# Attention over 32 heads: weighing the values in two halves of 256 columns, and the maxima seven steps ahead

## The chip, the core and the metric

The kernel is one program on one core of a Trainium2 chip. The metric is the device time of that program in microseconds (us). The core has five engines that run side by side and meet only at semaphores: TensorE (matmuls; PE in the rows, and PEld for its weight loads), VectorE (DVE), ScalarE (ACT), GpSimd (POOL) and SyncE (SP), which here issues the transfers. Matmuls write into PSUM, whose eight banks hold 512 float32 columns each.

## What is computed

Three layers follow each other on x of shape 2 x 2048 x 128: half a mixture-of-experts layer, attention with 16 heads of 8 dimensions in each of the 2 batches, and the mixture again. The change is in the attention:

```python
q = _rms_norm(q, q_norm_w); k = _rms_norm(k, k_norm_w)
q = _apply_rope(q, rope_cos, rope_sin); k = _apply_rope(k, rope_cos, rope_sin)
q = q / math.sqrt(HEAD_DIM)
scores = jnp.einsum('bqhd,bkhd->bhqk', q, k)
attn = jax.nn.softmax(scores.astype(jnp.float32), axis=-1)
out = jnp.einsum('bhqk,bkhd->bqhd', attn, v).reshape(b, s, HIDDEN)
return out @ wo.T
```

There are 32 heads (16 in each batch), each with 2048 queries and 2048 keys.

## The kernel before

`attention_phase` goes through the heads one after the other. A head is cut into 16 tiles of 128 keys (`KT`) and 4 chunks of 512 queries (`CHUNKS`, `BLK`). The softmax needs the maximum of each query's scores before it can take exponentials, so every score is computed twice. For the maxima the scores lie with queries on the partitions; for the weighing they lie with keys on the partitions.

A *step* g of a head is the inner loop of `turn` on TensorE. It issues, in this order, four pairs made of one scores matmul (`scores`, L1205; `pe_next`, L1250, for the first tile of the next head) and one maxima matmul (`maxima`, L1187), and then the weighing (`weigh`, L1215) of the key tile of the step before. The names used below are S0 to S3 for the scores of the four chunks, M0 to M3 for the maxima matmuls, and W for the weighing.

- S writes into a ring of three PSUM banks (`SRING`). ScalarE takes exponentials from there (`exps`, L1144) into `at_prob`, four a step. Sc may start once the exponential three entries earlier is done (`free`). So S3 waits for the exponential of S0 of its own step.
- M writes pairs of banks (`MRING` = 2 pairs). VectorE takes the maximum over each pair, 1024 columns at a time (`reduce`, L1275), two a step, 32 a head. M0 waits for the reduction of the pair two pairs earlier; so does M2.
- W multiplies the values of one key tile (`vals`, 128 x 32 float32, of which 8 columns are values and one gives the sum) by `at_prob`. Chunk c goes to the partitions 32c to 32c+31 of one bank, so that four matmuls of 512 columns work in four column groups of the array side by side. The bank O gathers all 16 tiles of a head. Each float32 matmul of the program is two matmul records in the trace, with a weight load each.

The maxima run ahead of the weighing. `LAG` = 11: in the steps 1 to 11 of head h TensorE issues the maxima of the tiles 5 to 15 of head h+1, and from step 12 on those of the tiles 0 to 4 of head h+2. When the last maxima of head h+1 are reduced, VectorE takes the maximum over the pairs and negates it (L1289), GpSimd splits it in three bfloat16 parts (`split`, L1071 to L1077), TensorE turns these (`turn_maxima`, L1200) at the end of step `TURN_MAXIMA` = 13, ScalarE copies them to `at_mrows` (L1155) and SP moves them into the rows of `q_head` that S reads with the others (`place_maxima`, L1104). The first S of the next head, in step 16, waits for that transfer.

At the end of a head ScalarE copies the bank O to `at_sums` (`keep_sums`, L1149) as soon as the last weighing is done. The first weighing of the next head waits for this copy. SP loads head h+3 and stores the sums of head h after the last weighing of head h. Before step 1 of head 0 there is a prologue with all 64 maxima matmuls of head 0 and the first 20 of head 1. In head 30 no maxima are left after step 11, and head 31 has none; in its steps 8 to 15 it also holds the output projection of the first batch.

Of the kernel before, what the change touches and what calls it, by code (L numbers as in the profile page):

```python
# [24 lines left out]
BLK = 512  # L25
# [11 lines left out]
HD1 = HD + 1  # L37
BH = BATCH * HEADS
PATCH = 508
KT = SEQ // P  # L40
LN_EPS, RMS_EPS = 1e-5, 1e-6
BUFS = 3
PROBS = 4
# [949 lines left out]
def attention_phase(nc, sem, kept, ps, v, identb, q, k, vals, q_rows, k_rows, qk_loaded, qk_stored,  # L993
# [9 lines left out]
    CHUNKS = SEQ // BLK  # L1003
    STEPS = KT * CHUNKS
    PAIRS_OF_HEAD = STEPS // 2
    ENTRIES = STEPS + 1
    AHEAD, LAG = 2, 11
    TURNS = BH - AHEAD
    SRING = 3
    MRING = 2  # L1010
    VSTEPS = 4
    TURN_MAXIMA = LAG + 2
    OUT_FROM = KT - 2 * BPS
    assert TURNS % BUFS == 0 and BUFS * ENTRIES % SRING == 0 and PAIRS_OF_HEAD % MRING == 0
    max_scored = sem("at_max_scored")
# [27 lines left out]
    with ExitStack() as tmp:  # L1043
# [56 lines left out]
        @block.sync  # L1100
        def _(sp):
            def place_maxima(h, i):
                sp.wait_ge(exped, turned_at(h) + 1)
                sp.dma_start(q[i][MROW:MROW + MR, :], mrows[:]).then_inc(max_placed, 16)  # L1104

            def store_sums(h):
                sp.wait_ge(sums_kept, h + 1 + PRIME)
                for c in range(CHUNKS):
                    cols = slice(c * BLK, (c + 1) * BLK)
                    sp.dma_start(sum_rows[h][:, cols], sums[32 * c:32 * c + HD1, :]).then_inc(sums_stored, 16)  # L1110

            def turn(h, i):
                place_maxima(h + 1, (i + 1) % BUFS)
                sp.wait_ge(weighed, (h + 1) * KT + PRIME)
                load_head(sp, q[i], k[i], q_rows[h + BUFS], k_rows[h + BUFS], qk_loaded[i])
                store_sums(h)

            prime(sp, sums_stored)
            for h in range(1, BUFS):
                load_head(sp, q[h], k[h], q_rows[h], k_rows[h], qk_loaded[h])  # L1120
            for i in range(2):
                sp.wait_ge(qk_stored[i], 16 * NB)
            place_maxima(0, 0)
            for it in range(0, BH // BUFS - 1):
                for i in range(BUFS):
                    turn(it * BUFS + i, i)
            for h in range((BH // BUFS - 1) * BUFS, BH):
                if h < BH - BUFS:
                    turn(h, h % BUFS)
                else:  # L1130
                    if h < BH - 1:
                        place_maxima(h + 1, (h + 1) % BUFS)
                    store_sums(h)
                if h == BH - 2:


                    load_sums(sp, 0, sum_rows, o, den, o_loaded[0])
# [42 lines left out]
        def _(pe):  # L1180
# [24 lines left out]
                pe.matmul(ps[:, S + bank(i, g, c, last), :], k[i][0:KS, g * P:(g + 1) * P],  # L1205
                          q[i][0:KS, c * BLK:(c + 1) * BLK], start=True, stop=True).then_inc(scored, 1)

            def weigh(h, i, g, last=False):

                pe.wait_ge(exped, entry(h, g, CHUNKS - 1, last) + 1)  # L1210
                if g == 0:
                    pe.wait_ge(values_placed, h + 1)
                    pe.wait_ge(sums_kept, h + PRIME)
                for c in range(CHUNKS):
                    last = pe.matmul(ps[32 * c:32 * c + 32, O, :], vals[i][:, g, :], prob[:, g % PROBS, c, :],  # L1215
                                     start=(g == 0), stop=(g == KT - 1), skip_group_check=True)
                last.then_inc(weighed, 1)

            def turn(h, i, loads=None, last=False):

# [2 lines left out]
                for g in range(1, KT + 1):  # L1223
# [4 lines left out]
                    for c in range(CHUNKS):  # L1228
# [4 lines left out]
                        if g <= LAG and not last:  # L1233
                            maxima(h + 1, nxt, (KT - LAG + g - 1) * CHUNKS + c)
                        elif g > LAG and loads is not None:
                            maxima(h + AHEAD, far, (g - LAG - 1) * CHUNKS + c)
                    if g == TURN_MAXIMA and not last:
                        turn_maxima(h + 1, nxt, turned_bank(i + 1))
                    weigh(h, i, g - 1, last)
                    if last and OUT_FROM <= g < KT:  # L1240
                        blk, part = divmod(g - OUT_FROM, 2)
                        if part == 0:
# [198 lines left out]
```

## Time and profile before

| | |
|---|---|
| median of 3 runs | 2074.75 us (2071.16 to 2346.2) |
| the profiled execution, its own time | 2068.4 us |
| its span | 2066.6 us |
| busy share of the span: PE, DVE, ACT, POOL | 89%, 74%, 63%, 16% |
| granted TensorE clock in the heads 1 to 30 | 1.00 of 2.4 GHz |
| maxima reductions (L1275) | 1024 of 1220 ns mean, 1206.5 us busy |
| exponentials (L1144) | 2048 of 604 ns mean, 1057.0 us busy |
| weighing matmuls (L1215) | 4096 records of 606 ns mean, 546.5 us busy |

A busy share is an average over the whole span. The attention heads take about 1,290 of the 2,066 us, and they are one pattern that repeats every step and every head, so it is read from a single step and a single head. Records of TensorE overlap: a matmul's duration includes its way through the array, and the distance from start to start says how long it holds the array.

### The profile page before, as it was taken

The page shows a single profiled execution, that of the slowest core. Times are in us where ns is not written, and L with a number is a line of the kernel's source. Part 1 is how long each engine was busy: PE and PEld are TensorE (multiplying, and loading weights), DVE is VectorE, ACT ScalarE, POOL GpSimd, SP SyncE. Part 2 cuts the span into 40 slices and gives each one's busy share as a digit, 9 for nine tenths or more (in the row PEclk, how much of TensorE's full clock was granted, in tenths as well). Part 3 has the DMA queues.
Part 4 walks back from the last instruction along what each step waited for, and adds up shares of the span by engine and source line. Part 5 has one row for each costly group of instructions (what it writes and reads, how often), then busy time and mean ns, then how long its engine had stood idle before and what let it go on. Part 6 is the DMA issues. An engine that isn't in the chain of part 4 may idle for free. (4 is left out here: it accounts for less than half of the span.)

```text
span 2066.6 us, 28460 instructions
## 1 busy us (share of the span) xinstructions
PE 1849.4 (89%) x10619; PEld 702.0 (34%) x10619; DVE 1520.4 (74%) x1691; ACT 1297.2 (63%) x2497; POOL 335.9 (16%) x408
## 2 busy tenths in 40 slices
PE   4799997689999999999999999999999997679998
PEld 2466655512222222222222222222222222456665
DVE  6333335599999999999999999999999972533333
ACT  3222223518888888888888888888888886222222
POOL 2355550300000000000000000000000000035554
PEclk9899996759999999999999999999999999689999
DMA  4543310300000000000000000000000001068462
GB/s 107 117 127 111 111 43 16 126 28 18 18 18 30 22 18 21 32 18 18 31 22 18 22 31 18 18 31 21 18 23 30 18 3 30 20 122 131 118 116 61
DMA packets 65155, 98.23 MB, mean 48 GB/s; under 512 B 12013, under 2 KB 31026, under 8 KB 65018
## 3 DMA queue, kind: packets, MB, share of 16 engines
q1 hardware_dynamic: 60858, 94.32, 18.0%
q10 hardware_dynamic: 4160, 2.10, 0.4%
q8 instruction: 84, 1.38, 0.3%
q14 instruction: 53, 0.43, 0.1%
HBM read 84.94 MB, written 11.04 MB: 46 GB/s over the span
## 5 line engine op out<-in xcount | busy, mean ns | idle before, releaser
L1275 DVE TENSOR_REDUCE at_mx<-ps 128x1 f32<-128x1024 f32 x1024 | 1206.5, 1220 | 78.1 <-PE ps L1187 39.8
L1144 ACT ACTIVATE at_prob<-ps 128x512 f32<-128x512 f32 x2048 | 1057.0, 604 | 215.4 <-PE ps L1205 203.1
L1187 PE MATMUL ps<-k_head,q_head 48*128 48x512 bf16 x2048 | 711.0, 395 | 20.4 <-PEq L779 14.1
L1205 PE MATMUL ps<-q_head,k_head 51*128 51x512 bf16 x1924 | 581.9, 383 | 75.0 <-ACT at_prob L1144 33.2
L1215 PE MATMUL ps<-at_prob,vals 128*32 128x512 f32 x4096 | 546.5, 606 | 0.0
L688 DVE TENSOR_TENSOR e_hidden<-e_part,ps 128x512 f32<-128x512 f32 (+1 forms) x208 | 143.2, 688 | 323.0 <-POOL e_part L665 318.2
L1205 PEld LDWEIGHTS ps<-q_head,k_head 51*128 51x128 bf16 x1924 | 143.4, 94 | 684.9 <-ACT at_prob L1144 574.1
L639 ACT ACTIVATE e_silu<-ps 128x512 f32<-128x512 f32 (+1 forms) x208 | 124.2, 597 | 323.1 <-PE ps L597 323.1
L665 POOL TENSOR_TENSOR e_part<-e_silu,e_cw 128x512 f32<-128x512 f32 (+1 forms) x208 | 264.5, 1272 | 366.1 <-ACT e_silu L639 200.7
L1187 PEld LDWEIGHTS ps<-k_head,q_head 48*128 48x128 bf16 x2048 | 151.2, 94 | 193.0 <-DVE at_mx L1275 176.3
L605 PE MATMUL ps<-e_hidden,wdown 128*128 128x512 f32 (+1 forms) x416 | 214.5, 598 | 2.0 <-DVE e_hidden L688 2.0
L1071 POOL TENSOR_TENSOR at_mparts<-at_neg,at_zero 128x16 bf16<-128x16 f32 x32 | 7.0, 220 | 984.8 <-DVE at_neg L1289 984.8
L597 PE MATMUL ps<-xnT_hi,wgate_hi 128*128 128x512 f32 x208 | 148.6, 714 | 10.7 <-DVE e_hidden L688 7.6
L1215 PEld LDWEIGHTS ps<-at_prob,vals 128*32 128x32 f32 x4096 | 80.9, 108 | 111.5 <-issue 108.1
L605 PEld LDWEIGHTS ps<-e_hidden,wdown 128*128 128x128 f32 (+1 forms) x416 | 77.5, 189 | 25.4 <-DVE e_hidden L688 9.8
L597 PE MATMUL ps<-xnT_hi,wgate_lo 128*128 128x512 f32 x208 | 82.9, 399 | 0.0
L597 PE MATMUL ps<-xnT_lo,wgate_hi 128*128 128x512 f32 x208 | 81.9, 394 | 0.0
L597 PE MATMUL ps<-xnT_hi,wup_hi 128*128 128x512 f32 x192 | 76.3, 397 | 0.0
L597 PE MATMUL ps<-xnT_hi,wup_lo 128*128 128x512 f32 x192 | 76.0, 396 | 0.0
L597 PE MATMUL ps<-xnT_lo,wup_hi 128*128 128x512 f32 x192 | 75.1, 391 | 0.0
L597 PEld LDWEIGHTS ps<-xnT_hi,wgate_hi 128*128 128x128 f32 x208 | 39.5, 190 | 71.8 <-issue 49.6
L597 PEld LDWEIGHTS ps<-xnT_lo,wgate_hi 128*128 128x128 f32 x208 | 39.7, 191 | 35.2 <-issue 35.1
(171 smaller groups left out, 896.9 us busy)
## 6 DMA issues: line engine op xcount, KB each, us to landing
e_cw<-comb_rows SPq DMA_DIRECT2D x80, 256.0 KB, 4.2
e_cw<-comb_rows SPq DMA_DIRECT2D x32, 224.0 KB, 5.9
e_cw<-comb_rows SPq DMA_DIRECT2D x32, 192.0 KB, 5.0
q_head<-q_rows SPq DMA_DIRECT2D x64, 96.0 KB
k_head<-k_rows SPq DMA_DIRECT2D x64, 96.0 KB
e_cw<-comb_rows SPq DMA_DIRECT2D x32, 160.0 KB, 4.5
e_cw<-comb_rows SPq DMA_DIRECT2D x48, 96.0 KB, 3.5
e_cw<-comb_rows SPq DMA_DIRECT2D x32, 128.0 KB, 6.1
```

The source lines that it names most:

```text
L597: last = pe.matmul(ps[:, bank + i, :], w[wp][:, cols], xnT[xp][:, tokens], start=(m == 0), stop=(m == len(PASSES) - 1))
L605: pe.matmul(ps[:, Y, :], wdown[0:rows[c], c, :], hidden[0:rows[c], (par + c) % 2, :], start=(c == 0), stop=(c == CH - 1)).then_inc(downed, 1)
L639: act.activation(silu[0:rows[c], i, :], ps[0:rows[c], GATE + i, :], ACT.Silu).then_inc(silued, 1)
L665: pool.tensor_tensor(part[0:rows[c], i, :], silu[0:rows[c], i, :], cw[0:rows[c], c, :], ALU.mult).then_inc(weighted, 1)
L688: dve.tensor_tensor(hidden[0:rows[c], i, :], part[0:rows[c], i, :], up, ALU.mult).then_inc(hidden_ready, 1)
L1071: pool.tensor_tensor(mparts[i][:, 0, :], neg[i][:], zero[:], ALU.add).then_inc(max_split, 1)
L1144: act.activation(prob[:, g % PROBS, c, :], ps[:, S + bank(i, g, c, last), :], ACT.Exp).then_inc(exped, 1)
L1187: one = pe.matmul(ps[:, at, :], q[i][HALF:HALF + KR, (j // CHUNKS) * P:(j // CHUNKS + 1) * P], k[i][HALF:HALF + KR, c * BLK:(c + 1) * BLK] ...
L1205: pe.matmul(ps[:, S + bank(i, g, c, last), :], k[i][0:KS, g * P:(g + 1) * P], q[i][0:KS, c * BLK:(c + 1) * BLK], start=True, stop=True).th ...
L1215: last = pe.matmul(ps[32 * c:32 * c + 32, O, :], vals[i][:, g, :], prob[:, g % PROBS, c, :], start=(g == 0), stop=(g == KT - 1), skip_grou ...
L1275: dve.tensor_reduce(mx[i][:, j // 2, j % 2:j % 2 + 1], ps[:, at:at + 2, :].rearrange("p a t -> p (a t)"), AX.X, ALU.max).then_inc(max_redu ...
```

## The change

Each weighing becomes two halves. Half 0 is issued after the second pair of the step and half 1 at its end, where the whole weighing stood. Half 0 takes the chunks 0 and 1, half 1 the chunks 2 and 3. A chunk is cut in two pieces of 256 columns, and the four pieces of a half go to the four column groups, so a half is again four matmuls side by side, each of 256 columns instead of 512. In the bank O half 0 has the columns 0 to 255 of the four groups and half 1 the columns 256 to 511. Half 0 waits for the exponential of chunk 1 of the tile before, half 1 for that of chunk 3; only half 1 tells the others that the tile is weighed. The first half 0 of a head carries the wait for `at_sums`.

`store_sums` still issues four transfers, now of 256-column pieces, to put the columns back in order. `LAG` goes from 11 to 9, so that seven tiles (0 to 6) of the maxima run two heads ahead instead of five, and the prologue has 28 maxima matmuls of head 1 instead of 20. `TURN_MAXIMA` is `LAG` + 3 = 12, one step earlier than before and three steps behind the last maxima of the next head instead of two.

```diff
-    AHEAD, LAG = 2, 11
+    AHEAD, LAG = 2, 9
-    TURN_MAXIMA = LAG + 2
+    HALF_BLK = BLK // 2
+    TURN_MAXIMA = LAG + 3
@@
-                for c in range(CHUNKS):
-                    cols = slice(c * BLK, (c + 1) * BLK)
-                    sp.dma_start(sum_rows[h][:, cols], sums[32 * c:32 * c + HD1, :]).then_inc(sums_stored, 16)
+                halves = sum_rows[h].rearrange("d (a j t) -> j d a t", a=2, j=4)
+                for j in range(4):
+                    sp.dma_start(halves[j], sums[32 * j:32 * j + HD1, :].rearrange("d (a t) -> d a t", a=2)).then_inc(sums_stored, 16)
@@
-            def weigh(h, i, g, last=False):
-                pe.wait_ge(exped, entry(h, g, CHUNKS - 1, last) + 1)
-                if g == 0:
+            def weigh(h, i, g, half, last=False):
+                pe.wait_ge(exped, entry(h, g, 2 * half + 1, last) + 1)
+                if g == 0 and half == 0:
                     pe.wait_ge(values_placed, h + 1)
                     pe.wait_ge(sums_kept, h + PRIME)
-                for c in range(CHUNKS):
-                    last = pe.matmul(ps[32 * c:32 * c + 32, O, :], vals[i][:, g, :], prob[:, g % PROBS, c, :],
-                                     start=(g == 0), stop=(g == KT - 1), skip_group_check=True)
-                last.then_inc(weighed, 1)
+                for j in range(4):
+                    done_one = pe.matmul(ps[32 * j:32 * j + 32, O, half * HALF_BLK:(half + 1) * HALF_BLK], vals[i][:, g, :],
+                                         prob[:, g % PROBS, 2 * half + j // 2, j % 2 * HALF_BLK:(j % 2 + 1) * HALF_BLK],
+                                         start=(g == 0 and half == 0), stop=(g == KT - 1), skip_group_check=True)
+                if half == 1:
+                    done_one.then_inc(weighed, 1)
@@
+                        if c == 1:
+                            weigh(h, i, g - 1, 0, last)
                     if g == TURN_MAXIMA and not last:
                         turn_maxima(h + 1, nxt, turned_bank(i + 1))
-                    weigh(h, i, g - 1, last)
+                    weigh(h, i, g - 1, 1, last)
```

TensorE's order in a step of head 0, before. L1205 rows are S, L1187 rows M, and L1215 rows W:

```order
L1205 MATMUL ps<-q_head0,k_head0 128x512 [waits at_exped]
L1187 MATMUL ps<-k_head1,q_head1 128x512
L1205 MATMUL ps<-q_head0,k_head0 128x512 [waits at_exped]
L1187 MATMUL ps<-k_head1,q_head1 128x512 [waits at_max_reduced]
L1205 MATMUL ps<-q_head0,k_head0 128x512 [waits at_exped]
L1187 MATMUL ps<-k_head1,q_head1 128x512
L1215 MATMUL ps<-at_prob,vals0 32x512 [waits at_sums_kept,at_values_placed,at_exped]
L1215 MATMUL ps<-at_prob,vals0 32x512 x3
```

The same place in the changed kernel (its lines stand one further on), from S1 and M1 to the end of the step:

```order
L1206 MATMUL ps<-q_head0,k_head0 128x512 [waits at_exped]
L1188 MATMUL ps<-k_head1,q_head1 128x512
L1216 MATMUL ps<-at_prob,vals0 32x256 [waits at_sums_kept,at_values_placed,at_exped]
L1216 MATMUL ps<-at_prob,vals0 32x256 x3
L1206 MATMUL ps<-q_head0,k_head0 128x512 [waits at_exped]
L1188 MATMUL ps<-k_head1,q_head1 128x512 [waits at_max_reduced]
L1206 MATMUL ps<-q_head0,k_head0 128x512 [waits at_exped]
L1188 MATMUL ps<-k_head1,q_head1 128x512
L1216 MATMUL ps<-at_prob,vals0 32x256 [waits at_exped]
L1216 MATMUL ps<-at_prob,vals0 32x256 x3
```

Four matmuls of 256 columns now stand between the second and the third pair, with the wait for `at_sums` on the first of them, and four more where the four of 512 columns stood. The second place is the end of the step that turns the maxima, on TensorE, before:

```order
L1205 MATMUL ps<-q_head0,k_head0 128x512 [waits at_exped]
L1187 MATMUL ps<-k_head2,q_head2 128x512
L1200 MATMUL ps<-identb,at_mparts1 48x128 [waits at_max_split,at_exped]
L1215 MATMUL ps<-at_prob,vals0 32x512 [waits at_exped]
L1215 MATMUL ps<-at_prob,vals0 32x512 x3
```

And in the changed kernel:

```order
L1206 MATMUL ps<-q_head0,k_head0 128x512 [waits at_exped]
L1188 MATMUL ps<-k_head2,q_head2 128x512
L1201 MATMUL ps<-identb,at_mparts1 48x128 [waits at_max_split,at_exped]
L1216 MATMUL ps<-at_prob,vals0 32x256 [waits at_exped]
L1216 MATMUL ps<-at_prob,vals0 32x256 x3
```

Here only the distance from the last maxima of head 1 has changed, from two steps to three, and what follows the turned matmul is half a weighing. The order of the work on ScalarE and GpSimd is as before but for that one step; VectorE's order is the same.

## Rows read from the trace of the kernel before

**Rows 1.** Windows view, heads 1 to 30: stretch, us, busy by engine, clock, DMA.
```profile
500.00:1660.00 1160.00, 1077.24 (x7433) 256.55 (x7431) 1092.80 (x955) 973.16 (x1910) 33.77 (x145) 1.00 0.07 23
```

**Rows 2.** Timeline of one step: start, duration, engine, line, operation, count, idle before.
```profile
1000.29 0.39 PE L1205 MATMUL ps<-q_head,k_head 51*128 51x512 bf16 x1
...
1000.51 0.38 PE L1205 MATMUL ps<-q_head,k_head 51*128 51x512 bf16 x1
1000.52 0.38 PE L1187 MATMUL ps<-k_head,q_head 48*128 48x512 bf16 x1
...
1000.77 2.06 ACT L1144 ACTIVATE at_prob<-ps 128x512 f32<-128x512 f32 x4 [0.39 <-PE ps L1205]
...
1001.42 0.39 PE L1205 MATMUL ps<-q_head,k_head 51*128 51x512 bf16 x1
...
1001.74 1.06 PE L1215 MATMUL ps<-at_prob,vals 128*32 128x512 f32 x8
...
1002.74 0.39 PE L1205 MATMUL ps<-q_head,k_head 51*128 51x512 bf16 x1
```

**Rows 3.** Timeline of VectorE in two short stretches around the same step.
```profile
1000.96 1.22 DVE L1275 TENSOR_REDUCE at_mx<-ps 128x1 f32<-128x1024 f32 x1
```
```profile
1000.96 2.36 DVE L1275 TENSOR_REDUCE at_mx<-ps 128x1 f32<-128x1024 f32 x2
```

**Rows 4.** Timeline of VectorE over one head.
```profile
972.96 0.18 DVE L1289 TENSOR_REDUCE at_neg<-at_mx 128x16 f32<-128x32 f32 x1
973.14 2.35 DVE L1275 TENSOR_REDUCE at_mx<-ps 128x1 f32<-128x1024 f32 x2
976.29 9.71 DVE L1275 TENSOR_REDUCE at_mx<-ps 128x1 f32<-128x1024 f32 x8 [0.80 <-PE ps L1187]
986.24 26.89 DVE L1275 TENSOR_REDUCE at_mx<-ps 128x1 f32<-128x1024 f32 x22 [0.24 <-PE ps L1187]
```

**Rows 5.** Timeline of PE, head 31: a weighing's two sets, in two short stretches.
```profile
1734.01 0.64 PE L1215 MATMUL ps<-at_prob,vals 128*32 128x512 f32 x4
```
```profile
1734.46 0.61 PE L1215 MATMUL ps<-at_prob,vals 128*32 128x512 f32 x4
1735.00 0.38 PE L1332 MATMUL ps<-woT,at_oT 128*128 128x128 f32 x1
```

**Rows 6.** Windows view of two dense stretches of TensorE; columns as in the first group.
```profile
361.40:364.80 3.40, 3.35 (x30) 3.25 (x30) 2.56 (x5) 2.82 (x7) 2.40 (x2) 1.00 0.01 2
1001.42:1001.80 0.38, 0.38 (x6) 0.15 (x10) 0.38 (x1) 0.38 (x2) 0.00 (x0) 1.00 0.00 0
```

**Rows 7.** Timeline, late in one head: turned maxima, copy of the sums, last load.
```profile
974.47 0.22 PE L1200 MATMUL ps<-identb,at_mparts 128*48 128x128 bf16 x1 [0.48 <-POOL at_mparts L1077]
...
982.98 0.39 PE L1205 MATMUL ps<-q_head,k_head 51*128 51x512 bf16 x1
...
983.11 0.60 ACT L1149 ACTIVATE at_sums<-ps 128x512 f32<-128x512 f32 x1
```
```profile
990.04 0.28 SPq L977 DMA_DIRECT2D k_head<-k_rows  x1
```

**Rows 8.** Timeline of VectorE in the prologue.
```profile
424.24 25.94 DVE L1275 TENSOR_REDUCE at_mx<-ps 128x1 f32<-128x1024 f32 x22
450.10 0.17 DVE L1289 TENSOR_REDUCE at_neg<-at_mx 128x16 f32<-128x32 f32 x1
450.19 4.70 DVE L1275 TENSOR_REDUCE at_mx<-ps 128x1 f32<-128x1024 f32 x4
```

**Rows 9.** Timeline of ScalarE: first exponentials of step 1, heads 0, 1, 30, 31.
```profile
464.39 2.06 ACT L1144 ACTIVATE at_prob<-ps 128x512 f32<-128x512 f32 x4 [1.63 <-PE ps L1205]
```
```profile
502.32 2.06 ACT L1144 ACTIVATE at_prob<-ps 128x512 f32<-128x512 f32 x4
```
```profile
1665.85 2.06 ACT L1144 ACTIVATE at_prob<-ps 128x512 f32<-128x512 f32 x4
...
1705.56 2.06 ACT L1144 ACTIVATE at_prob<-ps 128x512 f32<-128x512 f32 x4
```

## The prediction, made before the changed kernel ran

> **What bounds the kernel now.** I read the windows view first, to see whether the heads are one pattern and at which clock. From 500 to 1660 us VectorE is busy for 94%, TensorE for 93% and ScalarE for 84% of the time, at the full granted clock of 1.00 [rows 1]. Three engines are nearly full, so no busy share names the bound. The reader has to go to one step and ask of each engine what ended its last wait.
>
> The timeline of one step shows a closed loop through TensorE and ScalarE. S0 starts at 1000.29 and its exponential at 1000.77, 0.48 us later, after 0.39 us in which ScalarE had nothing to do. S3 starts at 1001.42, 0.65 us after that exponential began, because it needs the bank that the exponential frees. W starts at 1001.74, 0.32 us after S3, and the next S0 at 1002.74, 1.00 us after W [rows 2]. The sum is 0.48 + 0.65 + 0.32 + 1.00 = 2.45 us, which is exactly the distance from S0 to S0. So the step is bound by this loop. ScalarE's own work is less: four exponentials take 2.06 us and follow each other at (2.06 - 0.60)/3 = 0.49 us, so 1.95 us a step. The duration of one, 0.60, is read from the copy of the same shape [rows 7].
>
> VectorE is close behind. One reduction takes 1.22 us and two take 2.36 us from the first start to the last end [rows 3], so the second starts 1.14 us after the first when nothing holds it up. Two of them are 2.28 us a step, against the loop's 2.45. The rest is short waits for M. Over a head the timeline shows two bigger ones, 0.80 us and 0.24 us [rows 4], and a head takes (1665.85 - 502.32)/29 = 40.12 us [rows 9]. If VectorE never waited, a head would take 32 x 1.14 + 0.09 for the final maximum (450.10 to 450.19 [rows 8]) = 36.6 us.
>
> **What the split costs TensorE.** The array's time goes by distances from start to start. A pair (S and M side by side, 1000.51 and 1000.52) holds it for 0.22 us (1000.29 to 1000.51 [rows 2]). A weighing has two sets of four records. The second set starts 0.45 us after the first (1734.01, 1734.46) and what comes behind it 0.54 us later (1735.00) [rows 5]. At 2.4 GHz, the clock of these rows, 512 columns twice over are 0.43 us. So the first set costs 0.43 + 0.02, the second 0.43 + 0.11, and going from M3 to W costs 0.32 where a pair costs 0.22, another 0.10.
>
> With 256 columns the streaming part of each set halves to 0.21 us and the rest stays. A half is then 0.24 + 0.33 = 0.57 us, with 0.10 ahead of it. The step is pair 0.22, pair with the way into a weighing 0.32, half 0.57, and the same again: 2 x (0.22 + 0.32 + 0.57) = 2.22 us. As it stands, without waits, it would be 3 x 0.22 + 0.32 + 1.00 = 1.98 us. The split therefore adds 0.24 us of array time to each step. It is hidden as long as 2.22 is less than what VectorE needs, 2.28.
>
> The Trainium skill (TensorEngine Tiling (Array Packing), section Key Properties) says that a change of the tiling mode drains the engine, which speaks against this change, since S and M use half the rows each and W four column groups: two changes a step become four. The trace agrees that a change costs something, 0.10 us each way here. If each of the two added changes cost a matmul's whole way through the array, 0.18 us (the 0.39 us of a record of 512 columns less 0.21 of streaming [rows 2]), the step would be 2.22 + 2 x 0.08 = 2.38 us and TensorE the bound, about 2022 us in all by the reckoning of the first rival below; by the rows it is 2.22.
>
> **What the split removes.** W was one piece of 1.00 us between S3 and the next S0, inside the loop. Now S3 comes 0.22 + 0.32 + 0.57 + 0.22 = 1.33 us after S0, and needs its exponential, done 0.48 + 0.65 = 1.13 us after S0. The wait is gone, and it stays gone by 0.20 us. What is left of the loop on TensorE is its own order, 2.22 us. Then VectorE is late next: M0 starts about 0.05 us after the reduction that frees its banks ends, M1 0.22 later, it takes 0.39, and after 0.05 more its own reduction can start, 0.71 in all. (0.05 is taken from M1, which ends at 1000.52 + 0.38 = 1000.90, and its reduction, which starts at 1000.96 [rows 2, 3].) Counted from the start of the first reduction that is 1.22 + 0.71 = 1.93 us, and VectorE is free for it after 2 x 1.14 = 2.28. So 0.35 us of lateness on TensorE cost VectorE nothing. TensorE makes up 1.14 - 1.11 = 0.03 us in every half step, which is 1 us in a head.
>
> **What comes once a head.** The turned maxima waited 0.48 us for GpSimd and cost VectorE most of its 0.80 [rows 4, 7]; with three steps instead of two they are ready before TensorE asks, and 0.2 to 0.3 us of array time remain. That is within the 0.35. The first half weighing of a head now stands 0.54 us behind S0, while the copy of the sums starts 0.13 us behind that S0 (983.11 against 982.98) and takes 0.60 [rows 7]; with 0.05 for the signal it lets TensorE go at 0.78. So a new wait of 0.24 us appears on TensorE; behind it queue S2, M2, S3, M3, and VectorE waits for these. It too is within the 0.35. If that cover were gone, the two would cost 0.5 us a head, 15 us in all. Loads: SP's last one of a head is issued at 990.04 [rows 7], 7 us into the head; it is wanted in step 10, more than 20 us in, where it was step 12. The four stores of the sums are four still. Nothing for either.
>
> **The ends.** Head 0 runs from 464.39 to 502.32, heads 1 to 29 from there to 1665.85, head 30 to 1705.56 [rows 9]. The prologue gets four more reductions, at (25.94 - 1.22)/21 = 1.18 us each [rows 8]: +4.7 us. Head 0: 37.9 to 36.6, -1.3. Heads 1 to 29: 1163.5 to 29 x 36.6 = 1061.4, -102.1. Head 30: 39.7 to 9 x 2.28 + 7 x 2.22 = 36.1, -3.6. Head 31 has no M, so only TensorE's 2.22 against 2.45 in 16 steps: -3.7. What LAG itself brings is the 4.7 us in front and the 0.48 us of waiting; it moves reductions and saves none.
>
> **The sum**: 4.7 - 1.3 - 102.1 - 3.6 - 3.7 = -106 us. From the profiled execution's own 2068.4 us that gives 1962; that execution lay 0.3% under the median of 2074.75, the lowest run at 2071. I add 4 us for small hold-ups that I have no row for, and say 1966.
>
> **The rivals.** *The halves cost more than the rows say.* No row shows four column groups with 256 columns, whose weights (four loads a set) have 0.21 us instead of 0.43 to get in. The margin is only 0.03 us per half. Beyond it TensorE is the bound, and each 0.01 us more per half is 0.32 us a head, 10 us in all. With 0.05 more a head is 16 x 2.32 = 37.1 plus about 0.5 for the two waits above, now uncovered: 37.6, and the time 1995. At 0.12 more the gain is nothing. For it speaks that the margin is thin; against it that the same array takes single records of 128 columns every 0.11 us with full weights, 30 matmuls and 30 loads in 3.4 us [rows 6]. The Trainium skill (TensorE: Matmul & The Clock Gate, section Back-to-back issue gap) has matmuls bound by an issue of about 62 ns each in one decode setting. Eight of them would be 0.50 us a half against 0.45 of sets, which is this rival at +0.05, about 1995; no row decides it, since the records wait in a queue.
>
> *TensorE's issue becomes the bound, and the kernel is slower.* A step has 32 records (16 matmuls, 16 loads) now and will have 48. At more than 2.45/48 = 0.051 us for each, sustained, the step is longer than today. The densest long stretch has 60 in 3.4 us, 0.057 each [rows 6]: 48 would be 2.72 us, a head 43.5 and the time 2068 + 31 x 3.4 = 2174. Against it: 16 records are noted in the 0.38 us behind S3's wait, 0.024 each [rows 6], though these may have been queued before; and the 3.4 us hold 30 matmuls of 128 columns twice over, which at 2.4 GHz are 0.107 us each and account for the stretch by streaming.
>
> *The wait moves and the step stays.* If VectorE could not take a reduction every 1.14 us in a row (the rows show two, or four in 4.70 us with one longer distance [rows 8]), but only at the 1.22 of its duration, a head would be 32 x 1.22 + 0.1 = 39.1 and the time about 2068 - 31 = 2037. Against it: 22 in 25.94 us in the prologue, 1.18 each.
>
> **How the numbers follow.** As forecast, bound by VectorE, 1950 to 1980: 0.62. Halves dearer by 0.01 to 0.1, 1980 to 2045: 0.20. Reductions not at 1.14, 2000 to 2040: 0.07. Issue-bound and slower, 2070 to 2180: 0.07. Something unseen that keeps the time as it is: 0.04. The likeliest case alone is 1950 to 1980. The range goes to 2035, which leaves out the slower rival, no change and the worst of the dearer halves, about 0.15. Its low end is VectorE at 1.13 us a reduction, 10 us less, and no hold-ups. 2%, 41 us, is about what can be told from no change, so faster means under about 2033: 0.62 + 0.16 + 0.04 = 0.82; same 0.10; slower 0.08.
>
> **What would show it.** In the profile after: S0 to S0 is 2.28 to 2.30 us; VectorE over 98% busy in the heads, its reductions 1.14 us apart in long rows; S3 no longer waits for the exponential, M does wait for the reductions, which is where its idle time goes; half weighings 0.24 + 0.33 us. I am wrong if the sets of a half lie further apart, if VectorE still has a gap in each step, or if the wait for `at_sums` reaches VectorE.

## The result, and the profile after

The changed kernel takes 1964.13 us (median of 4 runs, 1960.59 to 1968.55), the kernel before 2072.95 us in the same series. The ratio is 0.9486 with a 95% interval of 0.9452 to 0.952; it leaves out one slow execution of the kernel before, 2346.2 us. The forecast was 1966 us with a range of 1950 to 2035. The profiled execution took 1963.15 us with a span of 1961.4, against 2066.6 before.

From the head of the page of the changed kernel: busy time, share and instructions of each engine, then VectorE's busy share and TensorE's granted clock in tenths over 40 slices:

```profile
span 1961.4 us, 36652 instructions
PE 1818.1 (93%) x14715; PEld 716.9 (37%) x14715; DVE 1477.8 (75%) x1691; ACT 1335.2 (68%) x2497; POOL 336.1 (17%) x408
...
DVE  6333335679999999999999999999999933623333
...
PEclk9899997856999999999999999999999997699999
```

The windows view over its heads (stretch, us, busy us and count of PE, PEld, DVE, ACT, POOL, then clock, DMA share and GB/s), the counterpart of [rows 1]:

```profile
500.00:1560.00 1060.00, 1047.49 (x11199) 269.78 (x11197) 1057.77 (x960) 1012.54 (x1920) 33.95 (x145) 1.00 0.08 25
```

VectorE is busy for 99.8% of this stretch where it was busy for 94%. TensorE went from 93 to 99% and ScalarE from 84 to 96%. All three are nearly full, so again the busy shares do not say which one decides. The timeline of VectorE does:

```profile
966.29 0.17 DVE L1294 TENSOR_REDUCE at_neg<-at_mx 128x16 f32<-128x32 f32 x1
966.39 36.44 DVE L1280 TENSOR_REDUCE at_mx<-ps 128x1 f32<-128x1024 f32 x32
1002.75 0.17 DVE L1294 TENSOR_REDUCE at_neg<-at_mx 128x16 f32<-128x32 f32 x1
1002.84 36.44 DVE L1280 TENSOR_REDUCE at_mx<-ps 128x1 f32<-128x1024 f32 x32
1039.20 0.17 DVE L1294 TENSOR_REDUCE at_neg<-at_mx 128x16 f32<-128x32 f32 x1
```

All 32 reductions of a head stand in one row without a gap. Over the whole stretch from 500 to 1560 us the view of L1280 has VectorE waiting for TensorE once, for 0.28 us (ahead of the row at 1054.35). One takes (36.44 - 1.21)/31 = 1.136 us from start to start, and a head takes 1039.20 - 1002.75 = 36.45 us. Before, the same row was broken by waits of 0.80 and 0.24 us and by short ones in each step [rows 4].

TensorE's timeline shows the half step that replaces the long piece of [rows 2]:

```profile
1009.88 0.39 PE L1206 MATMUL ps<-q_head,k_head 51*128 51x512 bf16 x1
1009.88 0.39 PE L1188 MATMUL ps<-k_head,q_head 48*128 48x512 bf16 x1
1010.11 0.38 PE L1206 MATMUL ps<-q_head,k_head 51*128 51x512 bf16 x1
1010.11 0.38 PE L1188 MATMUL ps<-k_head,q_head 48*128 48x512 bf16 x1
1010.42 0.64 PE L1216 MATMUL ps<-at_prob,vals 128*32 128x256 f32 x8
1010.99 0.39 PE L1206 MATMUL ps<-q_head,k_head 51*128 51x512 bf16 x1
```

The distances are 0.23, 0.31 and 0.57 us, together 1.11. In this half step TensorE catches up behind the turned maxima's matmul (1005.77) and waits for nothing. Where it has caught up, the distance grows to 1.13 or 1.14, because M then waits for a reduction. S0 to S0 is thus 2.21 to 2.27 us, a little under the 2.28 to 2.30 that I had named. S3 no longer waits: the list of TensorE's waits from 500 to 1560 us has no exponential left, where it had 24.0 us in 85 waits of S before.

The time went as follows, by stretches of the two profiled executions. The bounds of the heads are the ScalarE rows that answer to [rows 9].

| stretch | before | after | difference | forecast |
|---|---|---|---|---|
| start to the first final maximum (450.10, 452.68) | 450.1 | 452.7 | +2.6 | 0 |
| from there to 464.39 and 471.81 | 14.3 | 19.1 | +4.8 | +4.7 |
| rest of head 0 | 37.9 | 34.1 | -3.9 | -1.3 |
| heads 1 to 29 | 1163.5 | 1057.4 | -106.2 | -102.1 |
| head 30 | 39.7 | 36.2 | -3.5 | -3.6 |
| head 31, to the copy of its sums | 45.5 | 42.1 | -3.4 | -3.7 |
| from there to the end | 315.5 | 319.9 | +4.4 | 0 |
| span | 2066.6 | 1961.4 | -105.2 | -106 |

The rows of ScalarE for the changed kernel from which the table is made:

```profile
471.81 24.60 ACT L1145 ACTIVATE at_prob<-ps 128x512 f32<-128x512 f32 x44 [0.88 <-PE ps L1206]
...
505.86 1.10 ACT L1145 ACTIVATE at_prob<-ps 128x512 f32<-128x512 f32 x2
```
```profile
1563.21 1.10 ACT L1145 ACTIVATE at_prob<-ps 128x512 f32<-128x512 f32 x2
...
1599.40 1.10 ACT L1145 ACTIVATE at_prob<-ps 128x512 f32<-128x512 f32 x2
...
1641.54 0.60 ACT L1150 ACTIVATE at_sums<-ps 128x512 f32<-128x512 f32 x1 [1.82 <-PE ps L1216]
```

### The profile page after: what moved, and what is told of

It is laid out like the page before. It is cut to its first block and busy times, and to the rows that moved or that the text cites. A ratio compares the mean times of both kernels' runs of the same rounds, so it can differ in the third digit from the quotient of the medians.

```text
span 1961.4 us, 36652 instructions
## 1 busy us (share of the span) xinstructions
PE 1818.1 (93%) x14715; PEld 716.9 (37%) x14715; DVE 1477.8 (75%) x1691; ACT 1335.2 (68%) x2497; POOL 336.1 (17%) x408
## 5 line engine op out<-in xcount | busy, mean ns | idle before, releaser
L1280 DVE TENSOR_REDUCE at_mx<-ps 128x1 f32<-128x1024 f32 x1024 | 1165.9, 1214 | 9.6 <-PE ps L1188 7.6
L1145 ACT ACTIVATE at_prob<-ps 128x512 f32<-128x512 f32 x2048 | 1097.7, 595 | 67.3 <-PE ps L1206 22.5
L1216 PE MATMUL ps<-at_prob,vals 128*32 128x256 f32 x8192 | 655.0, 391 | 13.4 <-ACT at_sums L1150 13.4
L1188 PE MATMUL ps<-k_head,q_head 48*128 48x512 bf16 x2048 | 638.9, 392 | 21.6 <-PEq L779 14.7
L1216 PEld LDWEIGHTS ps<-at_prob,vals 128*32 128x32 f32 x8192 | 162.2, 108 | 427.4 <-ACT at_prob L1145 412.7
L1206 PEld LDWEIGHTS ps<-q_head,k_head 51*128 51x128 bf16 x1924 | 117.6, 93 | 403.7 <-ACT at_prob L1145 388.1
L1188 PEld LDWEIGHTS ps<-k_head,q_head 48*128 48x128 bf16 x2048 | 120.0, 94 | 62.5 <-DVE at_mx L1280 44.8
L1064 POOL COPY vals<-v 128x128 f32<-128x128 f32 x32 | 9.2, 292 | 332.5 <-PE ps L1216 332.5
```

The lines of the kernel that those rows point to most:

```text
L1064: pool.tensor_copy(vals[i][:, :, 0:HD], head).then_inc(values_placed, 1)
L1145: act.activation(prob[:, g % PROBS, c, :], ps[:, S + bank(i, g, c, last), :], ACT.Exp).then_inc(exped, 1)
L1188: one = pe.matmul(ps[:, at, :], q[i][HALF:HALF + KR, (j // CHUNKS) * P:(j // CHUNKS + 1) * P], k[i][HALF:HALF + KR, c * BLK:(c + 1) * BLK] ...
L1216: done_one = pe.matmul(ps[32 * j:32 * j + 32, O, half * HALF_BLK:(half + 1) * HALF_BLK], vals[i][:, g, :], prob[:, g % PROBS, 2 * half + j ...
L1280: dve.tensor_reduce(mx[i][:, j // 2, j % 2:j % 2 + 1], ps[:, at:at + 2, :].rearrange("p a t -> p (a t)"), AX.X, ALU.max).then_inc(max_redu ...
```

## The experiments

The theory under test has three parts. The step before was a loop through TensorE and ScalarE with the weighing in it. Halving the weighing and moving one half forward opens that loop. What is left is VectorE's pace, with TensorE close behind it because each piece of weighing has a fixed cost. The rivals are that VectorE was the bound already and the gain came from maxima that run further ahead, that short pieces help in themselves, and that moving the weighing would have done without cutting it.

### The halves without the rest, and the rest without the halves

```diff
 split_only, against the changed kernel
-    AHEAD, LAG = 2, 9
+    AHEAD, LAG = 2, 11
...
-    TURN_MAXIMA = LAG + 3
+    TURN_MAXIMA = LAG + 2
 ahead_only, against the kernel before
-    AHEAD, LAG = 2, 11
+    AHEAD, LAG = 2, 9
...
-    TURN_MAXIMA = LAG + 2
+    TURN_MAXIMA = LAG + 3
```

> The changed kernel with LAG and TURN_MAXIMA set back to 11 and 13; only the weighing stays in halves. Theory (the halves take the weighing out of the loop between TensorE and ScalarE, and VectorE's reductions become the bound): nearly the whole gain stays, a head of 36.5 to 36.9 us, in all 1965 to 1972 us: 5 us less in the prologue, but the turned maxima are now wanted about 2.3 us earlier (they were ready 1.7 us before TensorE asked), so TensorE waits some 0.6 us a head, of which VectorE feels 0.2 to 0.4. Rival (the gain is from running the maxima further ahead, so that VectorE is never short): back to 2050 to 2075 us, 40 us a head.

> The kernel before with LAG 9 and TURN_MAXIMA 12 and the weighing in one piece. Theory: the step stays 2.45 us, a head loses at most the 0.48 us for which TensorE waited for the split maxima and the prologue gets 5 us longer: 2060 to 2078 us. Rival (running ahead is the gain): 1965 to 2000 us.

The halves alone took 1981.93 us, ratio 0.9553 (0.953 to 0.9577). The maxima alone took 2063.98 us, 0.9957 (0.9942 to 0.9972), inside the 2060 to 2078 expected. So the halves alone bring 91 us of 109, and the rest brings 9 us by itself (0.4%, small but outside the interval) and 18 us on top of the halves. The 18 are more than I had expected: 1981.93 lies above my 1965 to 1972. The timeline of VectorE with the halves alone:

```profile
942.50 0.17 DVE L1294 TENSOR_REDUCE at_neg<-at_mx 128x16 f32<-128x32 f32 x1
942.59 2.35 DVE L1280 TENSOR_REDUCE at_mx<-ps 128x1 f32<-128x1024 f32 x2
945.40 8.01 DVE L1280 TENSOR_REDUCE at_mx<-ps 128x1 f32<-128x1024 f32 x7 [0.47 <-PE ps L1188]
953.65 26.11 DVE L1280 TENSOR_REDUCE at_mx<-ps 128x1 f32<-128x1024 f32 x23 [0.24 <-PE ps L1188]
979.68 0.17 DVE L1294 TENSOR_REDUCE at_neg<-at_mx 128x16 f32<-128x32 f32 x1
```

and, of the same kernel, a TensorE row from the head before:

```profile
906.83 0.22 PE L1201 MATMUL ps<-identb,at_mparts 128*48 128x128 bf16 x1 [0.77 <-POOL at_mparts L1078]
```

TensorE waits 0.77 us for the split maxima, and VectorE has nothing to do for 0.47 + 0.24 = 0.71 us of the head, which is 37.18 us long. That is 0.73 more than 36.45. Over 30 heads it is 22 us, less 5 us for the shorter prologue 17, against 18 measured. I had expected VectorE to feel only 0.2 to 0.4 us of it.

### Which of the two numbers counts

```diff
 lag11_turn14, against the changed kernel (TURN_MAXIMA stays LAG + 3)
-    AHEAD, LAG = 2, 9
+    AHEAD, LAG = 2, 11
 lag10_turn13, against the changed kernel
-    AHEAD, LAG = 2, 9
+    AHEAD, LAG = 2, 10
```

> The changed kernel with LAG 11 as before the change, and the turned maxima still three steps behind the last maxima, so in step 14. Theory (what mattered of the second part of the change is only the distance of three steps; LAG itself just makes the prologue longer): no wait for the split maxima, 36.45 us a head, and four reductions less ahead of head 0: 1956 to 1962 us, if the transfer of the turned maxima lands before step 16, where it is wanted two steps after it is made instead of four. Rival (that transfer is then late): 0.3 us or more a head lost, 1970 us and up. Rival (maxima seven steps ahead are needed in themselves): as with the halves alone, 1982 us.

> The same between the two: LAG 10, turned maxima in step 13. Theory: 36.45 us a head and two reductions less in the prologue, 1959 to 1964 us. Rival (maxima seven steps ahead are needed in themselves): 1970 us or more.

LAG 11 with the turn in step 14 took 1973.56 us, 0.9521 (0.9505 to 0.9538). LAG 10 with the turn in step 13 took 1963.42 us, 0.9468 (0.9449 to 0.9487), the same as LAG 9. The list of TensorE's waits for LAG 11 (engine, line, waited for: us in all, times, longest) names the reason:

```profile
PE ps L1255 <- DMA q_head<-at_mrows: 10.4, 28, 0.5
```

The wait for the split maxima is gone, but the transfer of the turned maxima now lands late: step 16 waits 10.4/28 = 0.37 us for it. A head takes 37.09 us (final maxima at 932.33 and 969.42). This was the first rival of that run. So LAG is bound from two sides: the turn has to stand three steps behind the last maxima and three ahead of the next head. With 16 steps that makes LAG 10 the largest that fits. LAG 10 gives the same time with six steps ahead, so "seven steps ahead" is not needed in itself.

### Was VectorE the bound before, and is it now?

```diff
 before_short_reduce and after_short_reduce
-                dve.tensor_reduce(mx[i][:, j // 2, j % 2:j % 2 + 1], ps[:, at:at + 2, :].rearrange("p a t -> p (a t)"),
+                dve.tensor_reduce(mx[i][:, j // 2, j % 2:j % 2 + 1], ps[:, at:at + 2, :].rearrange("p a t -> p (a t)")[:, 0:768],
```

> The kernel before with reductions over 768 instead of 1024 columns; the maxima over the left-out 256 columns are not taken. Theory (the step of 2.45 us is the loop of TensorE and ScalarE, and VectorE only stands close behind it): the step stays at 2.45 us, though VectorE has a fifth less to do; at most 0.4 us a head goes from the waits at the turned maxima, and some 5 us in the prologue: 2050 to 2068 us. Rival (VectorE's pace was the bound before as well): 2.0 us a step or a little more, below 1900 us.

> The changed kernel with reductions over 768 instead of 1024 columns; the maxima over the left-out 256 columns are not taken. Theory (VectorE is the bound at 1.14 us per reduction and TensorE stands just behind it at 2.2 us a step): the step falls only to TensorE's own 2.20 to 2.26 us, plus about 0.5 us a head of waits, a head of 35.7 to 36.4 us, in all 1940 to 1960 us. Rival (TensorE has room and VectorE alone is the bound): the step follows the reductions, about 1.75 us or ScalarE's 1.95, a head of 31 to 32 us, 1810 to 1830 us.

The kernel before took 2054.91 us with short reductions, the changed one 1946.39 us (one run each, 2073 in the same series for the kernel as it was). ScalarE's timeline of the kernel before with short reductions shows that the step has not moved at all:

```profile
1001.54 2.07 ACT L1144 ACTIVATE at_prob<-ps 128x512 f32<-128x512 f32 x4 [0.39 <-PE ps L1205]
1003.99 1.58 ACT L1144 ACTIVATE at_prob<-ps 128x512 f32<-128x512 f32 x3 [0.39 <-PE ps L1205]
```

It is 2.45 us as before, with the same 0.39 us of waiting for S0, although VectorE now waits 0.57 us in each step. A head is 39.73 us. VectorE was not the bound. In the changed kernel the head goes from 36.45 to 36.16 us only:

```profile
918.41 0.18 DVE L1294 TENSOR_REDUCE at_neg<-at_mx 128x16 f32<-128x32 f32 x1
...
954.57 0.17 DVE L1294 TENSOR_REDUCE at_neg<-at_mx 128x16 f32<-128x32 f32 x1
```

With VectorE out of the way TensorE's rows stand 2.21 us a step apart, 16 x 2.21 = 35.4 us; the other 0.8 us come once a head, from the wait for `at_sums` and the turned maxima's matmul. So VectorE is the bound now by 0.3 us in 36, and a faster VectorE would bring no more than that in a head.

### The place and the size of the pieces

```diff
 whole_middle, against the kernel before
+                        if c == 1:
+                            weigh(h, i, g - 1, last)
...
-                    weigh(h, i, g - 1, last)
 halves_end, against the changed kernel
-                        if c == 1:
-                            weigh(h, i, g - 1, 0, last)
...
+                    weigh(h, i, g - 1, 0, last)
                     weigh(h, i, g - 1, 1, last)
```

> The kernel before with the weighing in one piece, but issued after the second pair instead of at the end of the step. Theory (what counts is that the weighing no longer stands between S3 and the next S0; the halves cost 0.24 us of array time on top): the old loop is gone, another opens, S3 to its exponential 0.49, the exponential 0.60, 0.05 to the weighing of the next step, 1.00 for it and 0.22 for S2, 2.36 us a step, so a head of about 38 us and 2000 to 2015 us in all. Rival (two short pieces are what helps, since one long piece keeps VectorE short wherever it stands): 2.45 us a step or more, 2060 us and up.

> The changed kernel with both halves at the end of the step, one behind the other: the pieces stay, their place is undone. Theory (the gain is that the time between S3 and the next S0 is shorter by the first half): the old loop is back and its weighing a little longer, 0.48 + 0.65 + 0.32 + 3 x 0.24 + 0.33 = 2.50 us a step, about 0.8 us a head more than with the maxima ahead alone: 2080 to 2105 us. Rival (shorter pieces help in themselves): below 2000 us.

Both halves at the end took 2071.16 us (one run, the kernel before 2069.98 beside it). The gain is gone, so shorter pieces do nothing by themselves. But the time lies below my 2080 to 2105: I had the halves in a row too dear. TensorE's rows put sixteen records where eight were:

```profile
1003.01 1.07 PE L1216 MATMUL ps<-at_prob,vals 128*32 128x256 f32 x16
1004.02 0.39 PE L1206 MATMUL ps<-q_head,k_head 51*128 51x512 bf16 x1
```

From the start of the weighing to the next S0 it is 1.01 us, against 1.00 for one piece [rows 2]; I had expected 1.05. The four sets of the sixteen records start at 1003.01, 1003.25, 1003.47 and 1003.68, so from the second on a set costs 0.22 and 0.21 us, its streaming alone. Twice as many matmuls and weight loads one behind the other cost nearly nothing. The step is 2.46 us and the head 39.80, against 39.72 with the maxima ahead alone, where I had expected 0.8 us more.

The whole weighing in the middle took 2123.36 us, ratio 1.0261 (1.0221 to 1.0301). It is slower than the kernel before, and my 2000 to 2015 was wrong. TensorE and ScalarE over one step:

```profile
1003.21 0.39 PE L1205 MATMUL ps<-q_head,k_head 51*128 51x512 bf16 x1
...
1003.63 2.06 ACT L1144 ACTIVATE at_prob<-ps 128x512 f32<-128x512 f32 x4 [0.66 <-PE ps L1205]
...
1004.77 1.06 PE L1215 MATMUL ps<-at_prob,vals 128*32 128x512 f32 x8
...
1005.77 0.39 PE L1205 MATMUL ps<-q_head,k_head 51*128 51x512 bf16 x1
```

S2 starts at 1003.21 and its exponential 0.42 us later. The exponential of S3 has to queue behind it, 0.49 later, and takes 0.60; 0.05 later the weighing of that tile may start, which takes 1.00 until the next S2. That is 0.42 + 0.49 + 0.60 + 0.05 + 1.00 = 2.56 us, the distance from 1003.21 to 1005.77. I had let the exponential of S3 start 0.49 us after S3 and forgotten that ScalarE was still at the one before. The whole weighing needs the exponential of chunk 3, the last of the step, and in the middle of the next step that is a tight wait. This shows what the cut is for: half 0 needs only the chunks 0 and 1, which are ready long before the middle, so it can stand there. It does not show that cutting is the only way. A whole weighing in the middle, but of the tile before that one, should find all its exponentials done, and `at_prob` has room for four tiles; no run tried it.

### The price of a piece

```diff
 quarters, against the changed kernel (sums stored and copied to match)
-                pe.wait_ge(exped, entry(h, g, 2 * half + 1, last) + 1)
+                pe.wait_ge(exped, entry(h, g, half, last) + 1)
...
-                                         prob[:, g % PROBS, 2 * half + j // 2, j % 2 * HALF_BLK:(j % 2 + 1) * HALF_BLK],
+                                         prob[:, g % PROBS, half, j * QUARTER:(j + 1) * QUARTER],
...
-                        if c == 1:
-                            weigh(h, i, g - 1, 0, last)
+                        if c < 3:
+                            weigh(h, i, g - 1, c, last)
 quarters_from_head_2: the same where this is 4, halves where it is 2
+    def pieces(h):
+        return 4 if h >= 2 else 2
 three_pieces: half 0 as it is, the chunks 2 and 3 as quarters behind the third and the fourth pair
...
-                        if c == 1:
-                            weigh(h, i, g - 1, 0, last)
+                        if c in (1, 2):
+                            weigh(h, i, g - 1, c - 1, last)
```

> The changed kernel with the weighing in four quarters of 128 columns per column group, one behind each pair. Theory (each piece has fixed costs that do not shrink with its columns: 0.10 us into it, 0.02 between its sets, 0.11 out of it): a quarter is 0.32 + 0.13 + 0.22 = 0.67 us from pair to pair, the step 2.68 us and TensorE the bound by far, with the waits once a head 43.5 us a head, 2170 to 2195 us in all. First rival (the costs shrink with the columns): still VectorE's 36.5 us a head, 1965 us. Second rival (four weight loads no longer get in beside 0.11 us of streaming): each quarter longer by 0.1 us or more, 2230 us and up.

> The changed kernel with its second half cut in two quarters of 128 columns, one behind the third pair and one behind the fourth; SP stores the sums in eight transfers instead of four. Theory (each piece has fixed costs, 0.24 us, and the clock stays up): 0.22 + 0.32 + 0.57 + 2 x (0.32 + 0.35) = 2.45 us a step, TensorE the bound, 39.8 us a head, 2055 to 2085 us. Rival (costs shrink with the columns): 1965 us. Rival (with more and shorter pieces the granted clock stays at 0.50 as with the quarters): near 4 us a step, above 2700 us.

> Quarters as in the run before, but only from head 2 on; heads 0 and 1 are weighed in halves, so that the clock has risen to 1.00 before the first quarter. Theory A (the half clock of the quarters' run was only never left): the clock holds, the step is 2.68 us and the head 43.5 us, 2160 to 2185 us. Theory B (the quarters' pattern itself takes the clock down): it falls to 0.50 within head 2, the step goes to 4.5 us, above 2900 us.

The quarters took 3123.83 us. That is in the range of the second rival (2230 us and up), but not for its reason, and none of the three theories foresaw what happened. The windows view tells it; the third number from the end of a row is the granted clock:

```profile
480.00:500.00 20.00, 20.00 (x181) 5.45 (x180) 11.03 (x9) 10.75 (x18) 0.00 (x0) 0.50 0.00 1
...
1000.00:2000.00 1000.00, 996.28 (x8824) 271.80 (x8822) 540.94 (x455) 536.00 (x909) 16.30 (x70) 0.50 0.04 13
```

The clock read 0.50 (1.2 GHz) in the prologue, as in the kernels before and after the change, and it stayed there until late in head 31, with TensorE busy for 99.6% of the long stretch. It rose at last in the steps that also hold the output projection, behind the third group of its matmuls (L1337; the groups at 2766.21 and 2779.07 had not raised it), and the quarters that followed kept it:

```profile
2791.93 2.08 PE L1337 MATMUL ps<-woT,at_oT 128*128 128x128 f32 x8
```
```profile
2790.00:2794.00 4.00, 4.00 (x27) 2.35 (x26) 0.00 (x0) 1.19 (x2) 0.00 (x0) 0.50 0.00 0
...
2795.00:2800.00 5.00, 5.00 (x60) 1.79 (x56) 1.76 (x5) 3.44 (x7) 0.00 (x0) 1.00 0.00 0
```

In the changed kernel the clock rises soon after the first weighing:

```profile
465.00:470.00 5.00, 4.71 (x22) 0.83 (x22) 3.44 (x3) 3.20 (x7) 0.00 (x0) 0.50 0.01 3
```
```profile
470.00:475.00 5.00, 5.00 (x50) 1.15 (x48) 4.17 (x4) 4.08 (x8) 0.00 (x0) 0.84 0.00 0
475.00:480.00 5.00, 5.00 (x60) 1.27 (x56) 5.00 (x6) 4.80 (x10) 0.00 (x0) 1.00 0.00 0
```

With quarters from head 2 on the kernel took 2198.53 us. The clock was 1.00 when they began and held at 1.00:

```profile
600.00:1700.00 1100.00, 1085.38 (x15957) 406.31 (x15955) 977.64 (x823) 963.54 (x1644) 29.12 (x125) 1.00 0.07 22
```

So theory A of that run was right about the clock: the pattern of quarters does not take it down, but started at 0.50 it did not get up from there in 31 heads. The time is 13 us above theory A's 2160 to 2185. Only one run of each stands behind this, on two different chips; that the clock rose within the first of the two runs, with quarters before and behind, speaks against the chip as the cause. What raised it is not shown. Now the price of a piece can be read at the full clock, in TensorE's timeline of the same kernel:

```profile
1000.51 0.43 PE L1223 MATMUL ps<-at_prob,vals 128*32 128x128 f32 x8
1000.87 0.39 PE L1211 MATMUL ps<-q_head,k_head 51*128 51x512 bf16 x1
1000.87 0.39 PE L1193 MATMUL ps<-k_head,q_head 48*128 48x512 bf16 x1
1001.18 0.42 PE L1223 MATMUL ps<-at_prob,vals 128*32 128x128 f32 x8
```

A quarter is 0.36 us to the next pair and 0.31 from there to the next quarter, together 0.67 to 0.68, where 0.67 was expected. The step is 2.71 us and the head 44.20, 0.7 more than expected. Three pieces took 2079.09 us, within the 2055 to 2085 expected; their head is 40.03 us and TensorE's step 2.46.

The fixed cost can be put together from the three sizes. From a piece's start to the next pair it is 1.00 us with 512 columns, 0.57 with 256 and 0.36 with 128. Streaming is 0.85, 0.43 and 0.21 of that, so 0.14 to 0.15 remain each time. With two halves in a row they are paid once. Together with the 0.10 on the way in, a piece that stands apart costs 0.24 us, and it belongs to the change between pairs and weighing, not to the number of matmuls.

### A variant from these

```diff
 lag10_two_queues, against the changed kernel
-    AHEAD, LAG = 2, 9
+    AHEAD, LAG = 2, 10
...
+                store_groups(sp, h, range(2) if h == BH - 1 else range(4))
...
+            act.wait_ge(sums_kept, BH + PRIME)
+            store_groups(act, BH - 1, range(2, 4))
```

> LAG 10 with the turned maxima in step 13, and the last head's sums stored by two engines, two groups each (SP and ScalarE), since the four stores in a row take SP 3.20 us at the end of the attention where they took 1.35. Theory: 36.45 us a head as in the changed kernel, two reductions less ahead of head 0 (2.4 us) and 1 to 1.6 us less between the last copy of the sums and the reciprocal: 1958 to 1962 us. Rival (the transfers' own time and not their issue sets that distance): no gain at the end, 1962 to 1965 us.

It took 1961.55 us, ratio 0.9474 (0.9459 to 0.949). That is 2.6 us below the changed kernel's median, but the two intervals overlap, so it is not shown to be faster. The distance it was made for did shrink. The stores of the last head in the changed kernel, and the two parts in this one:

```profile
1642.17 3.20 SPq L1111 DMA_DIRECT2D sum_rows<-at_sums  x4
...
1653.84 3.35 DVE L1376 RECIPROCAL at_inv<-at_den 64x512 f32<-64x512 f32 x1 [11.73 <-DMA op_o_second<-sum_rows]
```
```profile
1641.93 1.61 SPq L1044 DMA_DIRECT2D sum_rows<-at_sums  x2
1641.93 2.45 ACTq L1044 DMA_DIRECT2D sum_rows<-at_sums  x2
...
1652.54 3.35 DVE L1382 RECIPROCAL at_inv<-at_den 64x512 f32<-64x512 f32 x1 [10.67 <-DMA op_o_second<-sum_rows]
```

From the first store to the reciprocal it is 11.67 us in the changed kernel and 10.61 here, 1.1 us less.

## Why the prediction was right, step by step

**The loop.** Right, and shown: with VectorE relieved of a quarter of its columns the old step stays at 2.45 us, and with both halves back at the end it is 2.46.

**The half weighing.** 0.24 + 0.33 = 0.57 us with 0.10 ahead of it; measured 0.57 and 0.31 from the pair before, 1.11 for the half step as forecast. The sum was right, and so were its two sets, 0.24 and 0.33 (they start at 1009.31 and 1009.55, and the next pair at 1009.88). One part was put in the wrong place. I had counted 0.02 us for each change from one set to the next, and the halves in a row show that this costs nearly nothing from the second set on. All of the cost lies in going over to the weighing and back. The Trainium skill's rule that a change of tiling mode drains the engine (TensorEngine Tiling (Array Packing), section Key Properties) fits this; the runs put numbers to it, 0.10 us in and 0.14 out.

**VectorE as the next bound.** Right: 1.136 us a reduction, 36.45 us a head against 36.6, and for heads 1 to 29 this makes the 4 us by which they went lower than forecast. TensorE stands only 0.3 us a head behind it, as the margin of 0.03 us in each half step said.

**The waits once a head.** The wait for the split maxima is gone, as forecast. The wait for the copy of the sums came, and it is about twice the 0.24 us of the forecast:

```profile
1015.70 0.60 ACT L1150 ACTIVATE at_sums<-ps 128x512 f32<-128x512 f32 x1
...
1016.45 0.64 PE L1216 MATMUL ps<-at_prob,vals 128*32 128x256 f32 x8 [0.43 <-ACT at_sums L1150]
```

The row counts 0.43 us from the end of the last record. By the distances of the forecast it is 0.50: the half stands 1.04 us behind S0 (1015.41) instead of 0.54. The copy starts 0.29 us after S0, not the 0.13 that I took from the kernel before, because ScalarE was still at its exponentials (its row has no gap ahead of the copy), and from its end to the half it is 0.15 us, not 0.05. From 500 to 1560 us TensorE waits for the copy 29 times, and VectorE has one gap, so in 28 of them it does not feel it. The 0.35 us of cover that I had worked out is therefore too low. The two slips went opposite ways: with the wait right and the cover as I had it, the forecast would have had this wait reach VectorE, which I had named as a sign of being wrong. The 0.77 us in the kernel with the halves alone are beyond it.

**The ends.** The four added reductions cost 4.8 us against 4.7. Head 0 was a slip of reading of mine: the first row of [rows 9] is not step 1 but step 2, since the eight exponentials ahead of it are those of the steps 0 and 1. Fifteen steps were left and not sixteen, so the gain was 3.9 us and not 1.3. The four stores were the term I put at nothing, and it was wrong: their count is the same, but four of them take SP 3.20 us to issue where they took 1.35. Why is open. That a row is now in two pieces is not enough: the kernel with three pieces stores two pieces of 128 columns a row in 0.32 us each. Nor does their number decide: the quarters, with four pieces a row, take 3.33 us for the four stores, the halves 3.29 in a head. Within the heads nothing waits for that. At the end of the attention the second layer does, and the distance from the copy of the sums to the reciprocal went from 10.0 to 12.3 us. The remaining 2.6 us before and 2.1 us behind the attention are in stretches that the change does not touch. They differ from execution to execution: in the twelve profiled kernels with whole reductions the first final maximum starts anywhere from 447.98 us (LAG 11, turn in step 14) to 457.10 (halves alone), with the same code up to there, and from the reciprocal to the end it is 305.5 to 307.6 us. Why is open.

**The rivals.** The halves are not dearer than the rows said. TensorE's issue is not a bound at 0.057 us a record: the quarters at full clock run 80 records in 2.71 us, 0.034 each. Reductions do go at 1.14 us in a row. The 4 us that I had added for unknown hold-ups have no single thing behind them: the stores took 2.3 us and the stretches outside 4.7.

**Luck.** The mechanism is shown, but that -105.2 us came so close to -106 is in part luck. Head 0 and the heads 1 to 29 went 2.6 and 4.1 us lower than forecast, and the stretches ahead of and behind the heads took 2.6 and 4.4 us more, which I had put at nothing.

## What to carry to other kernels

When three engines are all 85 to 95% busy, write the loop of one step as a sum of distances from start to start, and ask which piece of work stands in it without having to. A piece can be moved ahead of its place only as far as its own inputs allow, and cutting it is a way to let the part with early inputs go first. The cut has a fixed price on TensorE wherever the array's use changes, so cut no finer than the next bound asks for: two pieces gained 5%, three (one run) lost all of it again, and one piece in the middle was 2.6% slower than none moved.

## What was unexpected of the hardware

The granted clock was at 1.2 GHz during the prologue in the four kernels where I looked (before, changed, and both with quarters), and in three of them it rose within some 10 us of the first weighing. In the kernel with quarters from the start it did not, in 2,270 us (470 to 2740) of which TensorE was busy for 99.6%, and the step took 4.5 us. It rose only at about 2795 us, behind matmuls of the output projection. In the kernel that began with halves the same quarters ran at 2.4 GHz through the heads, 2.71 us a step. So in these two runs a TensorE that was always busy did not bring the clock up, and a pattern under which it did not rise held it once it was up. Why is not shown. The two kernels are 925 us apart. A row of the windows view over the first heads shows the clock.
